# Reading passes of a graph network, with the groups of source blocks as the outer loop and the sums of a group kept in PSUM

## The reference

```python
x = _layernorm(x + _L0_gnn_ref(x, L0_gnn_W, edge_weight, src, dst))          # sums over dst of h[src] * weight
x = _layernorm(x + _L1_gnn_ref(x, src, dst, edge_attr_64, ...))              # sums over src of f_ij * Wxh[dst]
x = _layernorm(x + _L2_gnn_ref(x, edge_index, W1, b1, W2, b2))               # sums over dst of x[src]
x = _layernorm(x + _L3_gnn_ref(x, edge_index, weight, bias))                 # sums over src of xw[dst], with degrees
```

## Time and profile before

| | us |
|---|---|
| median of 3 runs (lowest to highest) | 10582.6 (10569.26 to 10613.57) |
| the profiled execution, its own time | 10580.5 |
| its span, first to last instruction | 10575.2 |
| PE, DVE, ACT, POOL busy | 8093.8, 7858.0, 4035.1, 3285.7 |
| mean granted TensorE clock | 0.934 |

### The profile page before, as it was taken

The page is one execution under the profiler, slowest core; times in us unless marked ns, Lnnn a source line. Parts: engine busy times, 40 slices in busy tenths (PEclk is TensorE's granted clock), DMA queues, the critical chain, the costliest instruction groups (busy, mean ns, idle before and its releaser), DMA issues. The chain is left out here.

```text
span 10575.2 us, 353742 instructions
## 1 busy us (share of the span) xinstructions
PE 8093.8 (77%) x120877; PEld 6735.9 (64%) x120877; DVE 7858.0 (74%) x16484; ACT 4035.1 (38%) x13465; POOL 3285.7 (31%) x3158
## 2 busy tenths in 40 slices
PE   0468888888888888875666666664799998788886
PEld 0346666666666666664656666664577776788886
DVE  0246666666666666667999999999777776888888
ACT  0224444444444444442000000000577775666665
POOL 0277777777777777730000000000000000000000
PEclk9979999999999999987999999998899999999998
DMA  9634444444444444442333333332233331233322
GB/s 406 272 109 131 131 131 131 130 135 130 130 130 130 130 130 130 130 125 79 137 139 139 132 133 139 138 131 85 89 113 113 111 111 69 94 110 111 111 106 86
DMA packets 472031, 1378.26 MB, mean 130 GB/s; under 512 B 189238, under 2 KB 283510, under 8 KB 421574
## 3 DMA queue, kind: packets, MB, share of 16 engines
q1 hardware_dynamic: 346006, 1100.15, 31.1%
q10 hardware_dynamic: 25872, 167.19, 3.9%
q0 software_dynamic: 100000, 109.00, 3.2%
HBM read 1086.88 MB, written 289.10 MB: 130 GB/s over the span
## 5 line engine op out<-in xcount | busy, mean ns | idle before, releaser
L763 POOL DMA_INDIRECT edge_rows<-f_rows,f_index x3125 | 3240.9, 1037 | 968.3 <-issue 905.2
L1149 ACT ACTIVATE x_msg<-ps 128x384 bf16<-128x384 f32 x5488 | 2029.7, 456 | 889.4 <-PE ps L1420 463.5
L557 DVE TENSOR_TENSOR x_sel<-iotab,x_pairs 128x896 bf16<-128x896 bf16 (+1 forms) x2058 | 1598.2, 777 | 558.6 <-PE ps L1252 342.0
L1031 ACT ACTIVATE f_msg<-ps,f_yew 128x64 f32<-128x64 f32 x4802 | 1054.6, 324 | 1474.7 <-PE ps L944 1458.5
L1432 PE MATMUL ps<-tab,x_hot 128*128 (+1 forms) x28812 | 1041.3, 196 | 589.3 <-DVE x_hot L1339 583.9
L1432 PEld LDWEIGHTS ps<-tab,x_hot 128*128 128x128 bf16 x28812 | 956.2, 100 | 675.1 <-issue 657.2
L1446 PE MATMUL ps<-x_msg,x_sel 128*128 128x64 bf16 (+1 forms) x19208 | 1065.7, 194 | 245.1 <-DVE x_low L1367 239.0
L1446 PEld LDWEIGHTS ps<-x_msg,x_sel 128*128 128x128 bf16 x19208 | 948.5, 98 | 310.7 <-issue 299.6
L1339 DVE TENSOR_SCALAR x_hot<-x_row,iota 128x896 bf16<-128x896 bf16 x2744 | 1106.5, 445 | 0.9 <-issue 0.9
L959 PE MATMUL ps<-f_msg,f_ysel 128*128 128x192 bf16 x9604 | 998.3, 257 | 110.5 <-issue 110.4
L1420 PE MATMUL ps<-tab,x_hot 128*128 (+1 forms) x9604 | 913.7, 246 | 182.2 <-DVE x_hot L1339 153.5
(11 more groups left out here) (165 smaller groups left out, 13427.7 us busy)
## 6 DMA issues: line engine op xcount, KB each, us to landing
x_row<-edge_row_dst SPq DMA_DIRECT2D x196, 1568.0 KB, 6.4
edge_rows<-zeros ACTq DMA_DIRECT2D x49, 3332.0 KB, 36.9
f_piece<-edge_rows SPq DMA_DIRECT2D x343, 476.0 KB
x_f<-edge_rows SPq DMA_DIRECT2D x98, 1666.0 KB, 9.9
f_yrow<-edge_row_src SPq DMA_DIRECT2D x686, 224.0 KB
x_row<-edge_row_src SPq DMA_DIRECT2D x98, 1568.0 KB, 6.3
edge_rows<-f_rows,f_index POOLq DMA_INDIRECT x3125, 2.2
f_ea<-in_ea SPq DMA_DIRECT2D x48, 896.0 KB
```

Of the source, the lines that this page charges most:

```text
L557: return dve.tensor_tensor(sel[:, :, :].rearrange("p c (e two) -> p c e two", two=2), iotab[:, 0:columns].rearrange("p (e two) -> p e two" ...
L763: pool.indirect_dma_start(out=rowbuf, out_offset=bass.IndirectOffsetOnAxis(ap=index[:, j:j + 1], axis=0), in_=rows[:, j, :], in_offset=Non ...
L1031: i = act.activation(msg[g % 2][:, c, 0, :], got[g % 2][:, c * D:(c + 1) * D], ACT.Copy, scale=yew[h][:, lo + c:lo + c + 1])
L1149: act.activation(msg[g % 2][:, 2 * b:2 * b + m, :, :].rearrange("p c k d -> p (c k d)"), got[b][:, 0:m * PARTS * D], ACT.Copy).then_inc(x_ ...
```

## The change

- `read_pass` runs over the 14 groups outside and the 49 ranges inside. The 49 ranges are seven runs of RUN = 7 steps; the steps of a run are written out, and loops on the chip go over the runs and the groups. The last run of a group is written apart.
- The sums of a group stay in four PSUM banks over all 49 steps. Per cell the scatter is one matmul of 192 columns (193, filtered, with the count): the parts lie side by side and are not added. At a group's end ACT copies the four banks to `kept`, PE clears them with four matmuls (`cleared`), and DVE adds the three parts with one reduce into `acc` (`collect`), later, after six more runs. `accumulate` and the memset of `acc` are gone.
- The table's blocks now change with every step. PE takes them from a view of `tab3` in bytes, at a register's value plus a constant (`piece`); in the last run of a group the whole address is a constant.
- One-hots, selections and messages have three buffers, taken as 0,1,0,1,0,1,2 in a run; filtered, `got` has three banks.
- SP loads four or three ranges' rows of one group: the index row in pieces of 1792 bytes, f_ij in pieces of 1904. A load is for the next run, when this run's steps 0 to 3, or 4 to 6, are done with the buffer.
- In the fused pass the index pairs have two tensors. The destinations' are stored as before; the sources' lie by group, so `store_by_group` writes 14 pieces of 28 bytes a partition, at the end of a round. ACT waits for the store before it overwrites `pair`.

```diff
+                        def store_by_group(w):
+                            wait(sp, e_pair, w, 1, 1)
+                            settle(sp)
+                            sp.dma_start(srcpair_d.rearrange("p (g w e) -> p g w e", g=GW, w=NW)[:, :, bass.ds(w, 1), :]
+                                         .rearrange("p g o e -> p g (o e)"),
+                                         pair[:, 0:NS, :].rearrange("p (g c) two -> p g (c two)", g=GW))\
+                                .then_inc(e_by_group.sem, 16)
...
+        RUN = 7
+        RUNS = NW // RUN
+        BUFFER = (0, 1, 0, 1, 0, 1, 2)
+        SPANS = ((0, 4), (4, 7))
+        VW = PARTS * D
+
+        WROW = 2 * PARTS * D * 2
+
+        def reach(eng, count, t, more, per=1):
+
+            eng.wait_ge(count.sem, t * per + count.at(CREDIT + more * per))
...
+                        def reload(t, g, w):
+                            for h in range(2):
+                                reach(sp, x_hot, t, SPANS[h][1])
+                                settle(sp)
+                                reach(sp, x_sel, t, SPANS[h][1])
+                                settle(sp)
+                                if filtered:
+                                    reach(sp, x_whole, t, SPANS[h][1])
+                                    settle(sp)
+                                load(g, w, h)
...
+                        def collect(g):
+                            dve.wait_ge(x_out.sem, g * BANKS + x_out.at(BANKS))
                             settle(dve)
-                            at = acc[:, g * CG:(g + 1) * CG, 0:W]
-                            dve.tensor_tensor(at, at, sums[g % 2].rearrange("p (c w) -> p c w", w=W), ALU.add)\
+                            dve.tensor_reduce(acc[:, bass.ds(g * CG, CG), 0:D],
+                                              kept[:, :, 0:VW].rearrange("p c (k d) -> p c d k", k=PARTS), AX.X, ALU.add)\
                                 .then_inc(x_acc.sem, 1)
...
+                        def piece(e, at, m):
+
+                            return flat[:, bass.ds(e + at * 2, m * 2)].bitcast(BF16)
+
+                        def gather(t, j, e):
+                            b = BUFFER[j % RUN]
+                            reach(pe, x_hot, t, j + 1)
+                            if filtered:
+                                reach(pe, x_whole, t, j - 1)
                                 settle(pe)
-                                for c in range(2 * b, min(2 * b + 2, CG)):
-                                    at = (c - 2 * b) * PARTS * D
+                                for c in range(CG):
                                     for m in range(2):
...
+                                        for k in range(PARTS):
+                                            o = pe.matmul(got[b][:, c * D:(c + 1) * D], hot[b][:, m, c, :],
+                                                          piece(e, m * VW + k * D, D),
+                                                          start=m == 0 and k == 0, stop=m == 1 and k == PARTS - 1)
...
+                            for c in range(CG):
+                                o = pe.matmul(sums[c // 2][:, c % 2 * V:(c % 2 + 1) * V], sel[b][:, c, :],
+                                              upper_half(msg[b][:, c, :]) if filtered else msg[b][:, c, :],
+                                              start=False, stop=last and (c % 2 == 1 or c == CG - 1))
+                            o.then_inc(x_sum.sem, 1)
...
+                        def rounds(g):
+                            with loop(pe, 0, RUNS - 1) as r:
+                                e = pe.snap(r * (RUN * WROW))
+                                run(step_of(pe, g, r), e, e + RUN * WROW)
...
+                            with loop(pe, 0, GW - 1) as g:
+                                run(step_of(pe, g, RUNS - 1), (NW - RUN) * WROW, 0, True)
+                                pe.wait_ge(x_out.sem, g * BANKS + x_out.at(BANKS))
+                                settle(pe)
+                                cleared()
+                                rounds(g + 1)
+                            run(step_of(pe, GW - 1, RUNS - 1), (NW - RUN) * WROW, None, True)
...
+                        def taken(g):
+                            act.wait_ge(x_sum.sem, g * NW + x_sum.at(CREDIT + NW))
+                            act.wait_ge(x_acc.sem, g * TAKEN + x_acc.at(CREDIT))
+                            settle(act)
+                            for b in range(BANKS):
+                                act.activation(kept[:, 2 * b:2 * b + cells_of(b), :].rearrange("p c e -> p (c e)"),
+                                               sums[b][:, 0:cells_of(b) * V], ACT.Copy).then_inc(x_out.sem, 1)
```

More of the change, by code:

```diff
@@ L1320, in _ @@
                         with under(sp, 0):
                             for h in range(2):
[L1322 to L1329 removed]
+                                load(0, 0, h)
@@ L1376, in accumulate, with run @@
                                 .then_inc(x_acc.sem, 1)
-                        def body(w, start, last):
-                            for g in range(GW):
-                                nw, ng = (w, g + 1) if g + 1 < GW else (w + 1, 0)
+                            if filtered:
+                                dve.tensor_copy(acc[:, bass.ds(g * CG, CG), D:D + 1], kept[:, :, VW:V]).then_inc(x_acc.sem, 1)
+                        def run(t, i, last=False):
+                            for j in range(RUN):
@@ L1404, in _ @@
-                            with loop(dve, 1, NW - 1) as w:
-                                body(w, False, False)
-                            body(NW - 1, False, True)
-                            accumulate(NW - 1, GW - 1)
-                            dve.wait_ge(x_acc.sem, x_acc.at(GW + GW * NW))
+                                for b in range(3):
+                                    o = dve.memset(msg[b][:, :, VW:V], 1.0)
+                                o.then_inc(x_msg.sem, CREDIT)
+                            first(0, 0, 0)
@@ L1410, in _ @@
+                            run(step_of(dve, GW - 1, RUNS - 1), GW * RUNS - 1, True)
+                            collect(GW - 1)
+                            dve.wait_ge(x_acc.sem, x_acc.at(CREDIT + GW * TAKEN))
                     @block.tensor
                     def _(pe):
-                        def gather(w, g):
-                            wait(pe, x_hot, w, g + 1, GW)
-                            for b in range(0 if filtered else BANKS):
-                                pe.wait_ge(x_msg.sem, w * (GW * BANKS) + x_msg.at(CREDIT + (g - 1) * BANKS + b + 1))
+                        flat = tab3[:, :, :, :].rearrange("p t k d -> p (t k d)").bitcast(mybir.dt.uint8)
@@ L1435, in gather @@
-                            i.then_inc(x_got.sem, 1)
-                        def scatter(w, g):
-                            wait(pe, x_sel, w, g + 1, GW)
-                            wait(pe, x_msg, w, (g + 1) * MB, GW * MB)
-                            wait(pe, x_acc, w, g - 1, GW, GW)
-                            settle(pe)
-                            for c in range(CG):
-                                for k in range(PARTS):
-                                    V = D if k else W
-                                    part = part_of(msg, rest, low, k, c, g, V) if filtered else msg[g % 2][:, c, k, :]
-                                    i = pe.matmul(sums[g % 2][:, c * W:c * W + V], sel[g % 2][:, c, :], part,
-                                                  start=k == 0, stop=k == PARTS - 1)
-                            i.then_inc(x_sum.sem, 1)
@@ new lines, in scatter, with cleared, run @@
+                            o.then_inc(x_sum.sem, 1)
+                        def cleared():
+                            for b in range(BANKS):
+                                pe.matmul(sums[b][:, 0:cells_of(b) * V], onesb[:, :], zerob[:, 0:cells_of(b) * V],
+                                          start=True, stop=False)
+                        def run(t, e, follow, last=False):
+                            for j in range(RUN):
+                                if j + 1 < RUN:
+                                    gather(t, j + 1, e + (j + 1) * WROW)
+                                elif follow is not None:
+                                    gather(t, RUN, follow)
+                                scatter(t, j, last and j == RUN - 1)
```

277 lines of the change are left out of this document (152 added, 125 removed).

## The result

The kernel before has a median of 10578.13 us (4 runs, 10569.26 to 10613.57), the changed one 10916.81 (4 runs, 10911.14 to 10921.48): a ratio of 1.0313, 95% interval 1.0289 to 1.0338. It is slower by 339 us, where 97 were forecast. The sign was right, the size three and a half times too small.

What follows compares the result with a forecast made beforehand. It took DVE to bound the filtered pass's quiet steps and POOL's scatters the fused pass. Filtered +103, last -78 and fused +72 gave +97 on 10580.5, so 10678 us, with an 8-in-10 range of 10275 to 10930.

Steps and rivals of the forecast that it cites:

- Filtered pass, +103: Filtered pass: computed addresses +56, group ends +39, reduce +13, memset gone -5.5, together +103 us.
- addresses free: Rival: computed gather addresses cost nothing, 3.10 us per filtered step, -243 in that pass, 10284 us in all; chance 0.20.
- Last pass without the reloads: Last pass: forecast -78 us, with steps of 1.89 or 1.81, edges, group ends and reduce, apart from 15 for reloads.
- group ends and loop edges: Last pass: loop edges 40 us for 30 before, group ends 39, reduce of a group 15.
- right behind: Last pass: PE alone would need 1.85 us per step, just under the 1.89 taken.
- the reload in part 5: Last pass: an 896 KB row load needs 4.6 to 5.9 us against 5.6 of slack; 15 us, bounds 0 and 60.
- a rival, priced at +45: Last pass: a wait for reloads takes the accumulate's place, 60 us for 15; no separate chance given.
- reloads (DMA x_row) release DVE: Sign that the forecast is wrong: DVE's waits end when loads of index rows land.
- The store by group, +72: Fused pass: the store's small pieces cost POOL 1.5 us in each of 48 rounds, +72 us, bounds 0 to 180.
- the 10750: Total in us if each short store piece counts twice, 3 us a round, making the fused-pass term +144.
- The clock in the filtered pass: Granted clock: taken to mostly hold, though PE stands idle some 1.5 us in every period.
- the clock's case: Rival: the granted clock falls to half in a third of the filtered steps, +230, 10908 us; chance 0.20.

Runs made afterwards that it cites:

- rows by group: Changed kernel with destination rows stored in group order, so a load reads one piece of 7168 or 5376 bytes per partition; 10583.74 us, ratio 1.0001.
- addresses used ahead: On top of rows by group, six one-column matmuls use the filtered gather's addresses before its wait for the one-hots; 11972.83 us on another chip, ratio 0.9777.
- four stores: Changed kernel with each fused-pass round's store by group issued four times, to four tensors; 12731.17 us on one chip, 11024.78 on another.
- the rows apart: Changed kernel with index-row loads reading 1792-byte pieces at each partition's own place in DRAM, with other numbers; 10587.48 us, ratio 1.0004.

## Why the prediction was wrong in size

1. *Filtered pass, +103: right in its terms, and closer in the sum than they are.* Steps with a register take 3.65 in the median, 3.68 in the mean (forecast 3.69), with constants 3.06 in the median (3.10); DVE waits for PE 590 times, 404.3 us in all. A group's first step is 2.0 us longer than the others in the mean and its last 1.1: 14 x 2.0 + 13 x 1.1 = 42 us (39). The reduce takes 1.69 us (1.6 to 1.95). The measured +109 stands beside +108.5, but 12 of the 109 go with late rows here too: with rows by group the waits for them are 4.0 us instead of 13.8, and the pass is only 96 us longer than before. The experiment with addresses used ahead shows the cause, and it says what the case "addresses free" would have given: 2208.0 us from first to last one-hot for 2415.1 before, -207 where that case had -243.
2. *Last pass without the reloads: right in the sum.* -72.5 less the reloads' 15 is -87.5; the kernel with rows by group has 1379.8 - 1468.5 = -88.7. The parts are less close: steps in its middle runs take 1.94 (1.89), some 30 us more, so the group ends and loop edges cost some 35 less than their 94. And VectorE waits for the scatter in 662 of the 686 steps, not in every second: PE, which the forecast had "right behind", is busy for 1284 of the 1380 us and sets most steps.
3. *The failed step is the reload in part 5*: "one of 896 KB in smaller rows should need 4.6 to 5.9: 15 us in all, bounds 0 and 60". It took 7.8, and the term was 322 us (1702.0 less 1379.8), over five times its own upper bound. The slack of three steps, 5.6 us, was worked out right, and so was the place of the wait; it was even a rival, priced at +45. Its sign, "reloads (DMA x_row) release DVE", is what the trace then showed, 89 times. Its landing was scaled by bytes from one row, from pieces of 12,544 bytes to pieces of 1792, and nothing in the trace of before showed what 128 partitions reading the same short piece do: 7.8 us where separate places need 4.8. The price also left out the clock: in the changed kernel's last pass it fell to 0.50 in 74 stretches, with rows by group in 7, and 243 us of waits went with 322 of time.
4. *The store by group, +72: wrong.* Nothing of it can be seen, nor of four stores, within the 46 us by which the fused passes differ anyway. POOL's long scatters beside the raw loads were read as the cost of small pieces; these stores at least hardly bring them: 175 of the 3125 scatters took over 1.3 us before, 167 with the store, 204 with four. The Trainium skill, "DMA: Bandwidth & Descriptors" (Specifications), has a write of under 512 B done as a read and a write back. The store's own packets are dearer than their bytes (28 bytes took 7 ns in the median, the 784 before took 39), but whether by a read and a write back no trace here shows. Nobody waits for this store, and the 10750 worked out from it did not come.
5. *The clock in the filtered pass: right that it holds* (0.98), though the case beside it gave the time that came.

Near-right terms of +108.5 and -87.5, a term of 72 that was nothing, and a term of 15 that was 322: that is the result. The range of 10275 to 10930 held the time by luck: its width came from the clock's case, which did not occur.

## What to carry to other kernels

When a loop is turned inside out, follow every load to its new shape: the size of a contiguous piece, how many partitions read the same one, and how many steps lie between the last use of a buffer and its refill; where a load's landing is close to its slack, the bound must be wide, since the wait repeats in every run and can take the clock with it. Where sums move from an engine to PSUM, the freed engine gained nothing here until the chain behind it was cut, by making the one-hots two steps ahead instead of one. An experiment that moves one instruction moves its neighbours' waits: look at its trace before you believe either theory.

## What was not expected of the hardware

- 128 partitions reading one place of DRAM: pieces of 12,544 bytes, 1568 KB in 6.4 us; pieces of 7168, 896 KB in 4.4; pieces of 1792, 896 KB in 7.8; the same pieces from 128 places, 4.8. Around one slow load of the changed kernel (9699 to 9709) the packets of 1792 bytes took 74 to 349 ns each (medians by half a microsecond), with the rows apart nearly always 74; the filter rows of 1904 bytes, which lie apart, took 79 in the filtered pass.
- Registers as addresses: with an addition of 32 ns between them two of the gather's matmuls started 0.11 us apart, without it 0.03, and only the first use of an address in a gather paid (six times in 42 matmuls).
- Stores in pieces of 28 bytes didn't slow POOL's indirect scatters: the mean of one is 1037 ns without them, 1035 with 1792 pieces a round, 1043 with 7168. What they slow is the transfer behind it: the scatters' packets of 2176 bytes took 99, 102 and 181 ns in the mean, which POOL's instructions don't show.
